# Rotary halves exchanged by transfers inside SBUF in batches 1 to 3, so that DVE multiplies the whole bank by cosine and sine without crossing partitions

## The reference, cut to what matters

```
x1, x2 = (x[..., :D // 2], x[..., D // 2:])
out = jnp.concatenate([x1 * cos - x2 * sin, x1 * sin + x2 * cos], axis=-1)
...
xq = apply_rotary_emb(xq)
xk = apply_rotary_emb(xk)
```

## Time and profile before

| | |
|---|---|
| median of 3 runs | 417.36 us (417.29 to 417.52) |
| the profiled execution | 417.26 us |
| its span in the profile | 415.3 us |
| PE busy | 389.9 us (94%) |
| DVE busy | 332.6 us (80%) |
| ACT busy | 228.6 us (55%) |
| POOL busy | 98.6 us (24%) |
| chain that ended last, share on PE, DVE, ACT | 72%, 14%, 5% |

### The profile page before, as it was taken

The page is one execution under the profiler, slowest core; times in us unless marked ns, Lnnn a source line. Parts: engine busy times, 40 slices in busy tenths (PEclk is TensorE's granted clock), DMA queues, the critical chain, the costliest instruction groups (busy, mean ns, idle before and its releaser), DMA issues.

```text
span 415.3 us, 8773 instructions
## 1 busy us (share of the span) xinstructions
PE 389.9 (94%) x3016; PEld 329.9 (79%) x3016; DVE 332.6 (80%) x967; ACT 228.6 (55%) x488; POOL 98.6 (24%) x134
## 2 busy tenths in 40 slices
PE   2889999999999999999999999999999999798995
PEld 2769798778899788778998858979776998567894
DVE  4999587589669679888998979889889787888753
ACT  4254613435654895065887645569763258983340
POOL 7465241324203303141213123120011121000101
PEclk9999999999999999999999999999999999999999
DMA  6992000100000000000000001010000000000000
GB/s 212 323 375 61 2 2 8 45 25 2 0 2 2 26 2 27 27 1 27 2 2 14 27 2 28 0 39 3 0 27 2 2 0 13 15 3 0 13 17 25
DMA packets 12090, 14.54 MB, mean 35 GB/s; under 512 B 1040, under 2 KB 10128, under 8 KB 12048
## 3 DMA queue, kind: packets, MB, share of 16 engines
q1 hardware_dynamic: 11232, 13.20, 9.7%
q10 hardware_dynamic: 816, 0.79, 0.6%
HBM read 12.94 MB, written 1.05 MB: 34 GB/s over the span
## 4 chain that ended last, share of the span: by engine, by line
PE 72%; DVE 14%; ACT 5%; issue 5%; POOL 1%; DMA 1%; POOLq 0%; SPq 0%; DVEq 0%; ACTq 0%
PE acc L474 13%; PE bank L393 12%; PE bank L447 6%; PE bank L560 6%; PE bank L627 5%; PE bank L424 5%; PE bank L612 4%; PE bank L549 3%; PE bank L450 3%; PE bank L461 3%; PE bank L500 2%; PE bank L432 2%; ACT xs L757 2%; PE bank L572 2%; PE bank L537 1%
## 5 line engine op out<-in xcount | busy, mean ns | idle before, releaser
L1161 POOL TENSOR_TENSOR q_T<-q_T,rope_t 128x512 f32<-128x512 f32 x32 | 43.3, 1353 | 104.3 <-DVE rope_t L870 104.3
L757 ACT ACTIVATE xs<-xs,xneg 128x256 f32<-128x256 f32 x128 | 54.3, 498 | 19.1 <-DVE xneg L1007 19.0
L474 PE MATMUL acc<-wo_s,a_T 128*128 128x256 f32 x256 | 60.1, 380 | 0.0
L393 PE MATMUL bank<-x_hi,wqkv_hi 128*128 128x256 f32 x144 | 45.9, 319 | 7.7 <-DVE wqkv_lo L842 7.7
L474 PEld LDWEIGHTS acc<-wo_s,a_T 128*128 128x128 f32 x256 | 46.7, 190 | 7.0 <-issue 1.8
L1007 DVE CUSTOM_DVE_ANT_0 xs<-bank,mask_s 128x256 f32<-128x256 f32 x128 | 46.1, 418 | 0.3 <-PE bank L549 0.2
L447 PE MATMUL bank<-v_s,p_near 128*128 128x129 f32 x256 | 41.7, 276 | 1.4 <-POOL p_far L1167 1.4
L393 PE MATMUL bank<-x_lo,wqkv_hi 128*128 128x256 f32 x144 | 41.3, 287 | 0.0
L393 PE MATMUL bank<-x_hi,wqkv_lo 128*128 128x256 f32 x144 | 41.2, 286 | 0.0
L447 PEld LDWEIGHTS bank<-v_s,p_near 128*128 128x128 f32 x256 | 36.2, 191 | 5.9 <-issue 2.9
L722 ACT ACTIVATE p_near<-bank 128x512 f32<-128x512 f32 x32 | 19.1, 598 | 39.2 <-PE bank L424 39.1
(11 more groups left out here) (144 smaller groups left out, 845.6 us busy)
## 6 DMA issues: line engine op xcount, KB each, us to landing
stage<-in_wqkv SPq DMA_DIRECT2D x5, 512.0 KB, 4.6
wo_s<-in_wo SPq DMA_DIRECT2D x1, 2048.0 KB, 11.8
y<-in_x SPq DMA_DIRECT2D x4, 256.0 KB, 2.7
ctx_s<-in_ctxT SPq DMA_DIRECT2D x4, 256.0 KB, 2.8
mask_s<-in_mask SPq DMA_DIRECT2D x4, 256.0 KB, 2.7
w_s<-in_w1T SPq DMA_DIRECT2D x1, 1024.0 KB, 11.7
w_s<-in_w2T SPq DMA_DIRECT2D x1, 1024.0 KB, 12.7
out_y<-stage SPq DMA_DIRECT2D x8, 128.0 KB, 1.7
```

Of the source, the lines that this page charges most:

```text
L393: ins = mm(ps, lhs[i], rhs[j], start=(k == 0 and n == 0), stop=(last and n == 2))
L474: ins = mm(acc[:, t, :], a_T[:, j % 2, m, t * P:(t + 1) * P], wo_s[:, 2 * j + m, :], start=(j == 0 and t == 0 and m == 0), stop=(j == PAIR ...
L757: activation(xs[:, t, m, m2, :], xs[:, t, m, m2, :], ACT.Exp, bias=xneg[:, t, m, m2:m2 + 1], scale=-1.0)\
L1161: g.tensor_tensor(dst, dst, rope_t[:, n % 2], ALU.add).then_inc(sig["rotated", 0], 1)
```

## The change

In batches 1 to 3 DVE no longer crosses partitions. It multiplies the whole bank by the sine into `rope_t` with one instruction of 128x512, and then by the cosine into `q_T` with another. SP waits for the first of the two and copies the lower half of `rope_t` into the upper half of a new buffer `rope_s`, and the upper half into the lower one, by two transfers of 64 partitions x 512 elements (128 KB each). POOL waits for the transfers as well and adds `rope_s` in place of `rope_t`. The rotations of batch 0 stay as they were. The table `ORDER` is another one, so operations of all streams stand in other places of the plan; their number and sizes are the same.

```diff
 ORDER = (
-    "rrrrrrrmrrsrssrrrmsmssrmmsmmrrmmmmmsmsscmmmssrrrrmmmmmmrmmmmmmcmmmscmmmmmssrsccrmmmmsscysmmmsmsxrmccxycmc"
...
+    "rrrrrrrmrsrrsssrrmrmssmrmrrmmmmcsssmmmmmmscmmmmssrmmmmmmmrmmmmcmmrrccrcmmxssccmssmrrmmmmssyrxrrmmmccmmyxs"
...
+        def swaps_before(n):
+
+            return len(range(PAIRS + 1 + (n - PAIRS - 1) % 2, n, 2))
...
+            def swap_halves(b, i):
+
+                n = b * (PAIRS + 1) + i
+                lower, upper = slice(0, HD // 2), slice(HD // 2, HD)
+                if n >= 2:
+                    sp.wait_ge(sig["rotated", 0], n - 1)
+                wait_for(sp, "roped", b, 3 * i)
+                for dst, src in ((lower, upper), (upper, lower)):
+                    sp.dma_start(rope_s[dst, n % 2], rope_t[src, n % 2]).then_inc(swapped[n % 2], 16)
...
-                if kind == "quant_w" and i == 1:
+                if kind == "rot" and b:
+                    swap_halves(b, i)
+                elif kind == "quant_w" and i == 1:
...
+                if b:
+                    if n >= PAIRS + 3:
+                        dve.wait_ge(swapped[n % 2], 32 * swaps_before(n))
+                    v.tensor_tensor(rope_t[:, n % 2], ps, s, ALU.mult).then_inc(sig["roped", 0], 1)
+                    v.tensor_tensor(dst, ps, c, ALU.mult).then_inc(sig["roped", 0], 2)
+                    return
                 v.tensor_tensor(dst, ps, c, ALU.mult).then_inc(sig["roped", 0], 1)
...
                 wait_for(pool, "roped", b, 3 * i + 2)
-                g.tensor_tensor(dst, dst, rope_t[:, n % 2], ALU.add).then_inc(sig["rotated", 0], 1)
+                if b:
+                    pool.wait_ge(swapped[n % 2], 32 * (swaps_before(n) + 1))
+                g.tensor_tensor(dst, dst, (rope_s if b else rope_t)[:, n % 2], ALU.add).then_inc(sig["rotated", 0], 1)
```

More of the change, by code:

```diff
@@ L130, with work_streams @@
 ORDER = (
-    "rrrrrrrmrrsrssrrrmsmssrmmsmmrrmmmmmsmsscmmmssrrrrmmmmmmrmmmmmmcmmmscmmmmmssrsccrmmmmsscysmmmsmsxrmccxycmc"
[L132 to L135, removed]
-def make_plan():
[L140 to L148, removed]
+    "rrrrrrrmrsrrsssrrmrmssmrmrrmmmmcsssmmmmmmscmmmmssrmmmmmmmrmmmmcmmrrccrcmmxssccmssmrrmmmmssyrxrrmmmccmmyxs"
+    "smymmssymmmmyxsmmyxxysyxmrmmmmyymmmmmmrrxxrrmmxyxxxxsssyyymmymxmxyyyxxxyxymmmrrxyyxsyxmyxxmmsssyrrxccyxmm"
+    "mmscsmcyymmmnxmmmssnyxrccmmsxmmnmnyxmmnxrryxxmoyyxxxryyyryoxyxxxxyynxxxxyryoyxxxyyyxyyymxxymyycxcmmyxmmmm"
+    "msssmxccscymmoxycoxnssmmmyrryooysxmmmyymmxxmmssrrxyyyyxxxmmoxyxyymymyxmxxxyxyyxxmmyoxyxyxysnxysxsxyyccmmm"
+    "mmmxymmxymmmmmmmcnxccooynnxycxynnxyxyooxxyyxxyxxyxxxxyyxxxxyyyxxxnyyxyyyxonyyyxnnyxyxyoonyyonnooonnnoonoo")
+def work_streams():
+    every = range(B)
+    return {"c": [op for b in every for op in context_ops(b)],
+            "x": [op for b in every for op in cross_ops(b, 0)],
+            "y": [op for b in every for op in cross_ops(b, 1)],
+            "n": [op for b in every for op in network_ops(b, 0)],
+            "o": [op for b in every for op in network_ops(b, 1)],
+            "m": [op for b in every for op in mix_ops(b)],
+            "s": [op for b in every for op in score_ops(b)],
+            "r": [op for b in every for op in rotate_ops(b)]}
+def make_plan():
+    streams = work_streams()
     ops = {name: iter(stream) for name, stream in streams.items()}
@@ L211, in build_decoder @@
         x_hi, x_lo = sb("x_hi", [CK, T], F32R), sb("x_lo", [CK, T], F32R)
-        rope_t = sb("rope_t", [2, 2, T])
+        rope_t, rope_s = sb("rope_t", [2, 2, T]), sb("rope_s", [2, 2, T])
         q_T = sb("q_T", [4, 2, T])
@@ L270, in build_decoder @@
         wo_in, ffn_in, route_in = sem("wo_in"), sem("ffn_in"), sem("route_in")
+        swapped = [sem(f"swapped{i}") for i in range(2)]
         piece_hi, piece_lo = sem("piece_hi"), sem("piece_lo")
```

## The result

The changed kernel takes 418.63 us (median of 10 runs), the kernel before 417.55 us on the same chips: the ratio is 1.0025, with a 95% interval of 1.0017 to 1.0033. It is slower by about 1.1 us. The forecast was 412.8 us, and faster. The profiled execution took 418.99 us, with a span of 417.1.

A forecast was written before the change was run, and what follows sets the result against it. PE was taken as the bound between 60 and 340 us (98.7% busy), DVE second. Gains of 2.8 (DVE's relief) and 1.7 us (new order), less 0 for lag, took 417.26 to 412.8 us; range 407 to 418.8.

The forecast's parts named there:

- The cost is 0, hidden by that work: Later rotations in batches 1 to 3 cost 0, since other PE work ahead of each `near` covers them.
- the tightest place: Batch 3, pair 4: 5.6 us of PE work ahead of the `near`, against 4.6 us for the rotation.
- The terms for SP and POOL: SP's queue holds a swap back by at most 0.37 us; POOL's wait delays roots by 0, upper bound 1-2 us.
- PE's idle time in the middle: Between 60 and 340 us, forecast to fall from 3.7 to about 1 us; growth would show the prediction wrong.
- The lag: A rotation of batches 1 to 3 takes 4.6 us instead of 3.5, so ends 1.1 us later (0.6 to 1.6).
- an estimate of 3.3 us for the pair's landing: From the skill page's fixed cost and 196 GB/s: both swap transfers land at about 3.3 us, rotation ending at 5.3.
- my 2.6: Landing of the swap's two transfers, in us after SP is released: the middle of bounds 2.1 and 3.1.
- DVE's relief: Four rotations of batches 1 to 3 on the chain each lose one 0.69 us DVE instruction: 2.8 us gained.
- The moved end: Between 340 and 400 us, batch 2 network blocks fill a quarter of PE's 6.8 us idle: 1.7 us gained.
- The sum: Whole kernel: 2.8 + 1.7 - 0 = 4.5 us gained, from 417.26 to 412.8 us.
- The second: Rival: moved blocks hold back tile 1 at the end, 4 us lost against 2.8 gained, about 419 us; chance 0.13.
- The first: Rival: the swap becomes a new wait, at batch 3, pair 4's `near` and in DVE; about 421 us; chance 0.12.

The follow-up runs named there:

- x6: The changed kernel with full transfers that POOL doesn't wait for, POOL adding `rope_t` at once (halves not exchanged in batches 1 to 3): 416.18 us against 417.58.
- x7: The changed kernel with POOL's sum of batches 1 to 3 cut to 32 of each head's 256 columns, its late start kept: 415.42 us against 417.58.
- x11: The full changed kernel, with POOL waiting before five of its 27 late sums until the DVE instruction under each has ended: 417.40 us against 417.45.
- x3: The changed kernel, new order, without transfers or waits for them; POOL adds `rope_t` as it stands: 416.33 us against 417.56.
- x4: The changed kernel with the old `ORDER`, without transfers or waits for them; POOL adds `rope_t` as it stands: 416.24 us against 417.56.
- x9: The changed kernel with POOL summing `rope_t` at once, plus an unneeded POOL addition over scratch once each swap has landed: 421.82 us against 417.45.
- x5: The changed kernel with each transfer cut to 4 KB, POOL still waiting for both but adding `rope_t`: 419.72 us against 417.58.

## Why the prediction was wrong

**The step that failed** is "The cost is 0, hidden by that work". For the scores it was right: the tightest place, forecast to keep 1.0 us of slack, has 0.94 us in the trace, and PE waits for no rotation in batches 1 to 3. The terms for SP and POOL were right as well: DVE's waits for roots are still 0.7 us at the longest. But I asked only who needs the result of the late sum, and not what else runs while it runs. Before, the sum began 0.08 us behind DVE's last product, so it lay over DVE's next work, too, but in batches 1 to 3 the order was one in which no such instruction was held; in batch 0 three were, of which the prediction says nothing. Moved on to 2.5 us behind the last product, it fell on splits, quantising steps and the router's threshold, which have no operand in PSUM. The runs put +2.3 us in place of the 0. x6 and x7 show that it is neither the bytes nor the late start but the long sum at its late place, x11 takes half of it away by moving five sums later still, and PE's starts beside those of x3 put the loss behind four of the held instructions. The prediction had named as a sign of being wrong that PE's idle time in the middle grows: it did, from 3.7 to 5.4 us.

**The lag.** Forecast 4.6 us (4.1 to 5.1) from the first product's start to the sum's end; measured 5.0 to 5.2 at 20 of the 27 rotations, and 5.4 to 7.1 at the others. Each transfer lands 2.3 us after issue, and SP issues the second 0.5 us behind the first, not 0.37, so the pair lands 2.9 us after the first issue and the sum begins at 3.0. From the Trainium skill, "SBUF — State Buffer", sections "Door 1: The DMA port swizzle" and "The DMA setup-cost knee", the prediction had worked out an estimate of 3.3 us for the pair's landing; the measured 2.9 lies midway between that and my 2.6.

**DVE's relief.** Forecast -2.8 us, measured -1.3 us (x4). The size is off: four rotations on the chain at 0.69 us each gave less than half of it. That PE had queued work beside them is my reading, and no run shows it place by place. In x4 PE's idle time between 60 and 340 us goes from 3.7 to 3.1 us only:

```profile
60.00:340.00 280.00, 276.91 (x2169) 233.97 (x2168) 212.47 (x671) 164.84 (x356) 62.27 (x83) 1.00 0.05 13
```

**The moved end.** Forecast -1.7 us, measured 0: x3 is within 0.1 us of x4, and its last stage has 63.01 us of PE busy in 74.5, 11.5 us idle against the 11.4 of before. The filled gaps opened elsewhere. The rows of 360 to 380 and 380 to 400 us, first of x4 with the old order, then of x3 with the new:

```profile
360.00:380.00 20.00, 16.58 (x192) 13.38 (x191) 17.61 (x66) 13.96 (x37) 0.00 (x0) 1.00 0.01 2
380.00:400.00 20.00, 18.79 (x142) 17.27 (x141) 14.49 (x48) 6.85 (x12) 2.20 (x4) 1.00 0.04 14
```

```profile
360.00:380.00 20.00, 17.86 (x204) 15.12 (x205) 17.31 (x66) 13.77 (x36) 0.00 (x0) 1.00 0.01 2
380.00:400.00 20.00, 17.29 (x128) 15.41 (x127) 15.11 (x52) 7.00 (x13) 2.19 (x4) 1.00 0.04 14
```

PE's busy time rises by 1.3 us in the first and falls by 1.5 in the second.

**The sum** as measured: -1.3 + 0 + 2.3 = +1.0 us, against +1.1 seen. It closes because the three terms are steps from before to x4, x3 and the changed kernel; it is no check of them. None of my rivals had this mechanism. The second came nearest in time, about 419 us, but by luck: it had the moved blocks of the end lose, and x3 shows that the order loses nothing. The first was nearest by where it looked (the transfer as a new wait), but it named the wait of the scores.

## What to carry to other kernels

When a change moves a long POOL instruction in time, look at what DVE does in the new interval, not only at who waits for the result. In this kernel a DVE split, cast or quantising step that reads and writes SBUF stands still under a POOL sum, and it is booked as DVE busy time. The sign can stand in the trace of before, as one line whose instructions of one shape take two different times. Compare the durations of single instructions, not only their waits: the durations of the same tile before and after showed here what no wait did.

## What the runs showed of the hardware

- A POOL sum of 128x512 in SBUF holds a DVE TENSOR_TENSOR of 128x512 with two SBUF operands for as long as it runs: 1.64 us (75.40) to 1.78 (15.27 in batch 0) in place of 0.69, and 1.41 under the shorter idle sum of x9. Each of these ends 0.55 us behind the sum. It goes the other way, too: the sum at 14.71 us in the trace of before began 0.05 us behind a DVE split and took 1.79 us where 1.27 is its own. DVE products that read one operand from PSUM kept their 0.69 us. The Trainium skill, "SBUF — State Buffer", section "Who interferes with whom", has this as a lock on a port pair that DVE and GpSimd (POOL) share, taken by whichever starts first; the traces agree, with 1.67 us for the DVE instruction that began 0.15 us behind the sum, and 1.79 us for the sum that began 0.05 us behind the split.
- The sum also holds DVE instructions with one SBUF operand: casts (1.36 us for 0.43, L991 in x5) and TENSOR_SCALAR (1.24 for 0.17, line 1103). It doesn't hold every instruction that works in SBUF alone. A TENSOR_REDUCE of 128x256 kept its 0.41 us under two sums that run from 91.59 to 94.19:

```profile
92.36 0.41 DVE L938 TENSOR_REDUCE q_amax<-y 128x1 f32<-128x256 f32 x1
```

- A fill on POOL, which reads nothing, leaves such a TENSOR_TENSOR at 0.69 us and stretches a CAST to 1.09 us.
- Transfers inside SBUF of 64 partitions, 128 KB: 2.3 us from issue to landing; of 4 KB, 1.8 us. Their 7.1 MB beside all engines cost nothing (x6 is within 0.2 us of x3).
